# One attention and gated feed-forward layer: both chunks of the first sequence projected together through eight PSUM banks

## The chip, the cores and the metric

The kernel runs on one core of one Trainium2 chip. The metric is the device time of one execution in microseconds (us). Engines are named as the profile names them: PE (TensorE, matrix multiplications), ACT (ScalarE), DVE (VectorE), POOL (GpSimd), and SP, whose queue issues every DMA of this kernel.

## What is computed

Two sequences of 1024 tokens with 512 features are normalised, go through attention with 32 heads of 16 features (8 key/value groups) and, beside it, through a gated feed-forward layer with low-rank additions. The two results are multiplied and added to the input.

```python
x = L0_attn_x                                  # (2, 1024, 512), float32
xn = _layernorm(x, axis=-1)
s = attention(xn, Wq, Wkv, Wo, bo)             # causal, scores * 16**-0.5, softmax, context, Wo, + bo
gate = xn @ gate_w.T + (xn @ gate_a.T) @ gate_b.T      # 512 -> 1376, rank 16
up   = xn @ up_w.T   + (xn @ up_a.T)   @ up_b.T
hidden = silu(gate) * up
g = silu(hidden @ down_w.T + (hidden @ down_a.T) @ down_b.T)
out = x + s * g
```

## The kernel before, in words

**Precision.** Projections are made from a rounded high half and a low half of each operand: three matmuls (high by high, low by high, high by low; `matmul_hi_lo`, L240 to L242) for each 128 rows of the contraction. ACT writes the high half from a PSUM bank, DVE subtracts it from the value to get the low half.

**Tiling.** The 2048 tokens are four chunks `c` of 512 (0 and 1 are the first sequence, 2 and 3 the second). For a chunk there are: a layer norm on DVE (`layernorm`, L1239 to L1253) with one square root on ACT (`root`, L1031); four transposes `turn` (L809), of 4 blocks each; one projection for the keys (`KEYS_BLOCK`), four for the queries (`blk` 0 to 3), each of 12 matmuls of 512 columns; and `value` (L834), 16 small multiplications that the trace shows as 32 records. After a `turn`, ACT writes the unrounded `xT` (L1036, which `value` reads) and the high half `x_hi` (L1037), and DVE writes `x_lo` from them (L1259). Projections go to DRAM (`scratch_q`, `scratch_k`, L566) and values too (L571); they come back laid out for the heads (L738, L741, L745).

**Banks.** PSUM has eight banks of 512 columns: three for the scores `s`, two for the transposed scores `st`, one for the context `o`, and two (`bank0`, `bank1`) for everything that is not attention. `bank_places` hands these two out in turn; the next user of a bank waits (`take_bank`) until its last content was read, for a `turn` until `x_hi` is written, for a projection until `proj_lo` is.

**Order.** Each engine runs two streams: the background (turns, projections, values, then weights folded with their low-rank part in `fold` L847 and L851, then `hidden` L872, and later the output) and the attention, in 17 rounds of 40 slots. `interleave` first runs `LEAD` steps of the background alone, then gives so many steps to each slot. LEAD ended behind projection (1, 0), at step 36. Round -1 (the next 40 slots) takes another 30 steps (`EARLY`), and in it PE makes the scores of head group 0 (`score_pair`, L966, from slot 6 on) for the row maxima, which DVE takes (L1409 with the causal mask, L1412 without) and which are turned and stored as extra rows of `q` (L973, L753). With slot 0 of round 0 the transposed scores (L985) and the exponentials (L1191) begin. Behind round -1 every background step has its place by the same rule.

**The background's order up to there:** turn 0; then for chunks 0 to 3 the keys, the values, the turns of the next chunk, and one query projection (`BESIDE`); then two more query projections (`AFTER[:SOON]`), the two folds of the first weight tile, and `hidden`.

**Low-rank factors.** SP waits until all four values are stored (L658), then loads the raw factors `low_a_raw` and `low_b_raw` (L659, L660) into memory that the tiles of the first stage held, and behind them the first eight weight tiles (L594). ACT rounds both factors (`split_low`, L1058, L1059) and DVE takes their low halves (`low_of_low`, L1270, L1273). The first fold waits for both.

**The start of the attention.** SP's `LOAD` in slot 1 of round -1 waits until projections (0, 0), (1, 0) and the keys of chunk 1 are stored, then loads `k` and `q` of group 0 whole.

Of the kernel before, what the change touches and what calls it, by code (L numbers as in the profile page):

```python
# [80 lines left out]
LOAD = 1  # L81
# [13 lines left out]
PROJECTED = []  # L95
for _c in range(NCH):
    PROJECTED += [(_c, KEYS_BLOCK)] + BESIDE[_c:_c + 1]
PROJECTED += AFTER

# [10 lines left out]
SOON = 2  # L110
# [13 lines left out]
def bank_order():  # L124

    for k in range(KT):
        yield "turn", 0, k
    for c in range(NCH):
        yield "proj", c, KEYS_BLOCK
        yield "value", c, 0  # L130
        if c + 1 < NCH:
            for k in range(KT):
                yield "turn", c + 1, k
            yield ("proj", *BESIDE[c])
# [110 lines left out]
def layer(nc, x, Wq, Wkv, Wo, bo, gate_w, up_w, down_w, low_a, low_b, low_a_down, low_b_down, out):  # L245
# [5 lines left out]
    with ExitStack() as ctx:  # L251
# [35 lines left out]
        with ExitStack() as first:  # L287
# [6 lines left out]
            with ExitStack() as own:  # L294
                xT = sbuf(own, "xT", [P, KT, C])
# [7 lines left out]
            with ExitStack() as own:  # L303
                with ExitStack() as brief:
                    a_raw = sbuf(brief, "low_a_raw", [LR, 2, D])
# [3 lines left out]
                with ExitStack() as brief:  # L309
                    b_raw = sbuf(brief, "low_b_raw", [LR, 2, F])  # L310
                wh = sbuf(own, "w_hi", [P, 2, 2, KT, P], F32R)
                wl = sbuf(own, "w_lo", [P, 2, 2, KT, P], F32R)
                hid, hid_l = in_place(own, "hid", [P, 2, C], "_lo")
        x_in = ring[:, :, :].rearrange("p (a t) d -> p a t d", a=2)
# [45 lines left out]
        xT_hi = sem("xT_hi")  # L360
        xT_lo = sem("xT_lo")
        p_hi = sem("p_hi")
# [36 lines left out]
        loaded = [[sem(f"loaded{i}_{pair}") for pair in range(2)] for i in range(2)]  # L399
        v_loaded = [sem(f"v_loaded{i}") for i in range(3)]  # L400
# [25 lines left out]
        def bank_of(key):  # L426
            return bank[BANKS[key][0]]
# [7 lines left out]
        def read_out(kind, a, b):  # L435
# [4 lines left out]
            return dict(turn=(xT_hi, KT * a + b + 1), proj=(p_lo, (kind == "proj" and projection(a, b)) + 1), value=(v_copied, a + 1),  # L440
# [11 lines left out]

        def head_rows(h, n):
            return slice(64 * (h % 2), 64 * (h % 2) + n)
# [4 lines left out]
        def _(pool):  # L459
            pool.memset(prob[:, 0, 0], 0.0).then_inc(zero_made, 1)  # L460
# [46 lines left out]

            def background():
                done = 0
# [36 lines left out]
        def _(sp):  # L546
# [4 lines left out]

            def store_projection(c, blk):
# [3 lines left out]
                hi = ph[:, n % 2].bitcast(F32)  # L556
                lo = pl[:, n % 2].bitcast(F32)
# [16 lines left out]
            def load_raw(n):  # L574

                if n == 0:
                    wait_filled(sp, ("turn", NCH - 1, KT - 1))
# [64 lines left out]
            def background():  # L642
                yield KT * STEPS["turn"]
                load_x(2)
                for c in range(NCH):
# [4 lines left out]
                    if c + 1 < NCH:  # L650
                        yield KT * STEPS["turn"]
                        if c + 3 < NCH:
                            load_x(c + 3)
                        yield STEPS["proj"]
                        store_projection(*BESIDE[c])
                for i in range(2):
                    sp.wait_ge(v_stored[i], DMA * NCH // 2)
                sp.wait_ge(xn_ready, NCH)  # L658
                sp.dma_start(a_raw[:, :, :], low_a).then_inc(low_landed, DMA)  # L659
                sp.dma_start(b_raw[:, :, :], low_b).then_inc(low_landed, DMA)  # L660
                for n in range(8):
                    load_raw(n)
# [821 lines left out]
```

## Time and profile before

| what | us |
|---|---|
| median of 3 runs | 1012.03 (1011.39 to 1013.53) |
| the profiled execution | 1009.25 |
| its span, first to last instruction | 1007.5 |
| PE busy in the span | 925.6 (92%) |
| DVE / ACT / POOL busy | 584.2 / 486.1 / 304.1 |

The span is the time between the first and the last instruction of the profiled execution; 1.75 us of its time lie around it. Busy is the time in which an engine had at least one instruction running. A PE that is busy is not always at its full clock: the column PEclk of the table of windows gives the granted clock, 1.00 for 2.4 GHz and 0.50 for 1.2 GHz.

### The profile page before, as it was taken

The numbers are of one execution on the slowest core, as the hardware profiler recorded it, in microseconds if no ns is written. First come the engines' busy times: TensorE is split into PE (matmuls) and PEld (weight loads), VectorE is DVE, ScalarE is ACT, GpSimd is POOL, SyncE is SP. The second block draws the span as 40 slices with busy tenths as digits, with TensorE's granted clock in tenths as the row PEclk, the third lists the DMA queues.
The fourth block names the chain that finished last, engine by engine and source line by source line (L and its number), as shares of the span: only waits on it lengthen the run. The fifth ranks groups of instructions, "written<-read, shape, count | busy, mean of one in ns | idle before, by whom it ended". The sixth has DMA issues, their size and how long they took to land.

```text
span 1007.5 us, 18056 instructions
## 1 busy us (share of the span) xinstructions
PE 925.6 (92%) x6599; PEld 595.6 (59%) x6599; DVE 584.2 (58%) x1669; ACT 486.1 (48%) x975; POOL 304.1 (30%) x307
## 2 busy tenths in 40 slices
PE   4738699999999999999999999998999999989985
PEld 3625466666666666666666666554555555555664
DVE  6536656666666566665656575767655656640025
ACT  3402355656565556565656555656443443444211
POOL 3000023434343434343434343441111223120126
PEclk9967889999999999999999999999999999999999
DMA  6441724242424242424242433357745645335554
GB/s 230 150 110 44 248 86 136 76 143 79 141 81 133 84 129 86 122 87 122 90 117 96 120 100 116 91 143 218 204 116 157 178 143 141 91 94 155 156 158 151
DMA packets 142566, 129.01 MB, mean 128 GB/s; under 512 B 36104, under 2 KB 104296, under 8 KB 142256
## 3 DMA queue, kind: packets, MB, share of 16 engines
q1 hardware_dynamic: 142480, 127.87, 42.5%
q8 instruction: 54, 0.88, 0.4%
q14 instruction: 32, 0.26, 0.1%
HBM read 74.07 MB, written 53.22 MB: 126 GB/s over the span
## 4 chain that ended last, share of the span: by engine, by line
PE 79%; DVE 8%; DMA 4%; ACT 4%; issue 2%; SPq 2%; POOL 0%; POOLq 0%; DVEq 0%; ACTq 0%
PE bank L872 24%; PE o L1002 12%; PE bank L240 9%; PE s L966 9%; PE st L985 8%; PE bank L241 6%; PE bank L242 6%; DVE junk L1409 2%; PE bank L834 2%; DMA q<-scratch_q 2%; DVE neg_pad L1425 1%; PE bank L847 1%; PE bank L851 1%; DVE hid L1299 1%; DMA inv_sums<-scratch_r 1%
## 5 line engine op out<-in xcount | busy, mean ns | idle before, releaser
L1191 ACT ACTIVATE prob<-st 128x512 f32<-128x512 f32 (+1 forms) x640 | 324.3, 554 | 289.9 <-PE st L985 289.5
L1409 DVE CUSTOM_DVE_ANT_0 junk<-s,mask 128x128 bf16<-128x128 f32 (+3 forms) x512 | 229.4, 487 | 126.6 <-PE s L966 125.7
L1412 DVE TENSOR_REDUCE part_max<-s 128x1 f32<-128x512 f32 x256 | 163.7, 681 | 106.6 <-PE s L966 106.6
L484 POOL TENSOR_SCALAR_AFFINE_SELECT prob<-prob 128x512 f32<-128x512 f32 x128 | 84.2, 670 | 351.6 <-ACT prob L1191 351.1
L966 PE MATMUL s<-k,q 64*128 64x512 f32 (+3 forms) x768 | 150.3, 380 | 22.7 <-DMA q<-scratch_q 12.3
L872 PE MATMUL bank<-x_hi,w_hi 64*128 64x512 f32 (+1 forms) x704 | 151.0, 416 | 2.4 <-DVE hid L1299 1.1
L1002 PE MATMUL o<-prob,v 128*32 128x512 f32 (+3 forms) x1536 | 144.6, 494 | 0.0
L872 PE MATMUL bank<-x_lo,w_hi 64*128 64x512 f32 (+1 forms) x704 | 142.7, 392 | 0.0
L872 PE MATMUL bank<-x_hi,w_lo 64*128 64x512 f32 (+1 forms) x704 | 141.8, 390 | 0.0
L985 PE MATMUL st<-q,k 64*128 64x512 f32 (+3 forms) x768 | 136.6, 374 | 3.6 <-ACT prob L1191 3.6
L966 PEld LDWEIGHTS s<-k,q 64*128 64x128 f32 x768 | 77.4, 187 | 66.5 <-DVE part_max L1409 26.6
L493 POOL TENSOR_TENSOR tanh<-tanh,hid 128x512 f32<-128x512 f32 (+1 forms) x44 | 56.6, 1286 | 166.1 <-DVE hid L1299 166.1
L985 PEld LDWEIGHTS st<-q,k 64*128 64x128 f32 x768 | 71.8, 185 | 58.3 <-issue 35.1
L872 PEld LDWEIGHTS bank<-x_hi,w_hi 64*128 64x128 f32 (+1 forms) x704 | 68.7, 183 | 42.2 <-issue 32.2
L240 PE MATMUL bank<-down_hi,hid_in 128*128 128x512 f32 (+1 forms) x176 | 78.1, 444 | 2.9 <-issue 2.2
L501 POOL TENSOR_TENSOR hid_lo<-hid,tanh_hid_hi 128x512 fp32r<-128x512 f32 (+1 forms) x44 | 56.7, 1289 | 75.8 <-ACT tanh_hid_hi L1100 75.8
L1002 PEld LDWEIGHTS o<-prob,v 128*32 128x32 f32 x1536 | 39.5, 109 | 65.4 <-issue 61.3
L872 PEld LDWEIGHTS bank<-x_lo,w_hi 64*128 64x128 f32 (+1 forms) x704 | 68.6, 182 | 13.0
L872 PEld LDWEIGHTS bank<-x_hi,w_lo 64*128 64x128 f32 (+1 forms) x704 | 69.1, 183 | 7.5
L241 PE MATMUL bank<-down_lo,hid_in 128*128 128x512 f32 (+1 forms) x176 | 69.2, 393 | 0.0
L242 PE MATMUL bank<-down_hi,hid_in 128*128 128x512 f32 (+1 forms) x176 | 69.0, 392 | 0.0
L495 POOL TENSOR_TENSOR hid<-tanh,hid 128x512 f32<-128x512 f32 (+1 forms) x44 | 56.5, 1283 | 3.5
(103 smaller groups left out, 1004.1 us busy)
## 6 DMA issues: line engine op xcount, KB each, us to landing
hid_in<-scratch_hid SPq DMA_DIRECT2D x16, 1408.0 KB, 7.3
q<-scratch_q SPq DMA_DIRECT2D x64, 200.0 KB
scratch_hid<-tanh_hid_hi SPq DMA_DIRECT2D x40, 256.0 KB, 2.1
scratch_hid<-hid_lo SPq DMA_DIRECT2D x40, 256.0 KB, 2.4
scratch_q<-proj_hi SPq DMA_DIRECT2D x32, 256.0 KB
scratch_o<-o_sb SPq DMA_DIRECT2D x32, 256.0 KB
k<-scratch_k SPq DMA_DIRECT2D x32, 192.0 KB
scratch_q<-proj_lo SPq DMA_DIRECT2D x16, 256.0 KB
```

The lines of the kernel that those rows point to most:

```text
L240: pe.matmul(out, lhs_hi, rhs_hi, start=start, stop=False)
L241: pe.matmul(out, lhs_hi, rhs_lo, start=False, stop=False)
L242: return pe.matmul(out, lhs_lo, rhs_hi, start=False, stop=stop)
L484: ins = pool.affine_select(out=blk, in_=blk, compare_op=ALU.is_ge, fill=0.0, base=0, pattern=[[0, REP], [1, P]], channel_multiplier=-1)
L501: pool.tensor_tensor(hid_l[0:hp, n % 2], hid[0:hp, n % 2], hid_h[0:hp, n % 2], ALU.subtract)\
L872: mm = pe.matmul(bank[i][0:hp, :], w_[half, h % 2, i, kt, 0:hp], x_[half, c, kt], start=not cross and kt == 0 and w_ is wh and x_ is xh, s ...
L966: pe.matmul(sb_[(p + odd) % S_BANKS][:, 0:wd], q[half, g % 2, h // 2, qt * P:(qt + 1) * P], k[half, g % 2, k0:k0 + wd], start=True, stop=T ...
L985: mm = pe.matmul(st[odd][:, col:col + q1 - q0], k[half, i % 2, kt * P:(kt + 1) * P], q[half, i % 2, h // 2, q0:q1], start=True, stop=True)
L1002: mm = pe.matmul(ob[32 * h:32 * h + 2 * HD, q0 % C:q0 % C + q1 - q0], v[:, i % 3, kt].rearrange("p a e -> p (a e)"), prob[:, job % 3, h, c ...
L1191: nc.scalar.activation(prob[:, job % 3, h, 0:JOB_COLS[j]], st[at % ST_BANKS][:, 0:JOB_COLS[j]], ACT.Exp, scale=float(HD) ** -0.5).then_inc ...
L1409: ins = dve.tensor_tensor_reduce(junk[:, n % S_BANKS, 0:wd], bank_[:, 0:wd], mask[:, C - wd:C], 1.0, LOWEST, ALU.add, ALU.max, part[:, h, ...
L1412: ins = dve.tensor_reduce(part[:, h, qt, dst:dst + 1], bank_[:, 0:wd], AX.X, ALU.max)
```

## The change

- **Order.** `LEADING` is new: the turns of chunks 0 and 1, then keys and query block 0 of chunk 0 and of chunk 1, then the values of both. Behind it come, for chunks 2 and 3, the turns, one query projection of chunk 0 or 1 (block 1), the keys, the values. `SOON` goes from 2 to 1. LEAD ends behind the same projection (1, 0), which now is step 24; EARLY is 42 steps. The total is the same.
- **Banks.** The eight turns of chunks 0 and 1 take all eight banks, one each; DVE's `x_lo` is now made from the bank. A turn's bank is free when `xT` is copied, which for chunks 0 and 1 happens apart from the rounding and later (`round_x`, `copy_x`); `xT` has two halves for it.
- **POOL** takes over the low halves of the key weights, of the query weights (in four pieces, `low_query_weights`) and of `x` for chunks 2 and 3 (`low_x` in the POOL block). ACT rounds the query weights in four pieces.
- **Buffers.** The third and fourth projection (keys and block 0 of chunk 1) are written to the buffers of the exponentials (`prob`), which nothing uses at that time. So are the raw low-rank factors, loaded at the program's start. ACT rounds `bT` behind the square root of chunk 3 (`split_low_b`) and `low_a` once all values are stored (`split_low_a`).
- **Loads.** `x` of chunk 1 is loaded ahead of `wkv`. `load_first` brings the first 512 columns of `k` and `q` of group 0 as soon as chunk 0's two projections are stored; `LOAD` brings the rest, and the values of a group are loaded in slot 19 rather than slot 1. The first eight weight tiles are loaded four at a time, behind the turns of chunk 2 and of chunk 3.
- **Layer norms** of chunks 0 and 1 follow each other on DVE; chunk 2's stands behind the eight `x_lo`, chunk 3's behind `proj_lo` of (0, 0).

```diff
-LOAD = 1
+LOAD, LOAD_V = 1, 19
...
-BESIDE = [(0, 0), (1, 0), (0, 1)]
-AFTER = [(1, 1), (0, 2), (1, 2), (0, 3), (1, 3)] + [(c, blk) for blk in range(NBLK - 1) for c in (2, 3)]
...
+LEADING = [(c, blk) for c in range(2) for blk in (KEYS_BLOCK, 0)]
+BESIDE = {2: (0, 1), 3: (1, 1)}
+AFTER = [(0, 2), (1, 2), (0, 3), (1, 3)] + [(c, blk) for blk in range(NBLK - 1) for c in (2, 3)]
+PROJECTED = LEADING + [p for c in BESIDE for p in (BESIDE[c], (c, KEYS_BLOCK))] + AFTER
...
-SOON = 2
+SOON = 1
...
-    last, turn, places, prior = [None, None], 0, {}, {}
+    last, turn, places, prior = [None] * 8, 0, {}, {}
...
+        elif u < 8:
+            used = (u,)
...
+            def load_first():
...
+                for a in range(2):
+                    sp.wait_ge(p_stored[a], 3 * DMA)
+                sp.wait_ge(zero_stored, DMA * (B + 2))
+                for h in range(2):
+                    sp.dma_start(k[head_rows(h, ROWS), 0, 0:C].bitcast(F32), k_dram[0][:, 0:C]).then_inc(first_loaded[0], DMA)
+                for h in range(REP):
+                    sp.dma_start(q[head_rows(h, AUG), 0, h // 2, 0:C].bitcast(F32), q_dram[h][:, 0:C])\
+                        .then_inc(first_loaded[h // 2], DMA)
...
+            sp.dma_start(a_raw, low_a).then_inc(low_landed, DMA)
+            sp.dma_start(b_raw, low_b).then_inc(low_landed, DMA)
...
+            def split_low_a():
+                for i in range(2):
+                    act.wait_ge(v_stored[i], DMA * NCH // 2)
+                act.wait_ge(xn_ready, NCH)
+                nc.scalar.activation(a_gu[:, :, :], a_raw, ACT.Copy).then_inc(low_hi, 1)
...
+                for c, blk in LEADING:
+                    if c == 1 and blk == KEYS_BLOCK:
+                        root(3)
+                        split_low_b()
+                        for kt in range(KT):
+                            copy_x(1, kt)
+                    yield STEPS["proj"]
+                    split_projection(c, blk)
```

**ACT at the start.** Before, from the first square root to the first copy of the values; `small` is the square root, `xT` and `x_hi` are the two copies of a turned bank.

```order
L1031 ACTIVATE small<-small 128x4
L1118 ACTIVATE wk_hi<-wkv 128x512
L1036 ACTIVATE xT<-bank 128x512
L1037 ACTIVATE x_hi<-bank 128x512
...
L1031 ACTIVATE small<-small 128x4
L1124 ACTIVATE wq_hi<-wq 128x2048
L1045 ACTIVATE proj_hi<-bank 128x512
L1052 ACTIVATE v_sb<-bank 128x4x8x16
```

Now ACT, from behind the copies of chunk 0 to the projections of chunk 1, with the banks' numbers:

```order
L1100 ACTIVATE small<-small 128x4
L1125 ACTIVATE proj_hi<-bank0 128x512
L1125 ACTIVATE proj_hi<-bank1 128x512
L1100 ACTIVATE small<-small 128x4
L1138 ACTIVATE bT<-prob 96x2752
L1112 ACTIVATE xT<-s2 128x512
L1112 ACTIVATE xT<-st0 128x512
```

The square root of chunk 3, the rounding of `bT` and the last four copies now stand between the projections of chunk 0 and those of chunk 1.

**PE around the first scores.** Before, the scores begin beside the values of chunk 1:

```order
L834 MATMUL bank<-wkv,xT 128x128 x4
L966 MATMUL s<-k,q 128x128 x2
L834 MATMUL bank<-wkv,xT 128x128 x4
L966 MATMUL s<-k,q 128x256 x2
L966 MATMUL s<-k,q 128x384 x2
L834 MATMUL bank<-wkv,xT 128x128 x4
```

Now PE, at the same slots:

```order
L896 MATMUL bank<-wkv,xT 128x128 x28
L1035 MATMUL s<-k,q 128x128 x2
L896 MATMUL bank<-wkv,xT 128x128 x4
L1035 MATMUL s<-k,q 128x256 x2
L867 MATMUL bank<-ident,ring 128x128 x4
L1035 MATMUL s<-k,q 128x384 x2
```

Seven of the eight value steps of chunks 0 and 1 now stand ahead of the first score, and the turns of chunk 2 beside the next ones. From the first transposed scores (`st`) on, PE's rows are the same in both programs.

**DVE ahead of the folds.** Before, behind the last query projection of round -1 (`low_a`, `bT` are the low halves of the two factors):

```order
L1265 TENSOR_TENSOR proj_lo<-bank,proj_hi 128x512
L1270 TENSOR_TENSOR low_a<-low_a_raw,low_a 32x1024
L1273 TENSOR_TENSOR bT<-low_b_raw,bT 32x2752
L1409 ISA junk,part_max<-s,mask 128x512
```

Now DVE, at the end of the values of chunk 3:

```order
L1519 TENSOR_REDUCE part_max<-s 128x1 x2
L1380 TENSOR_TENSOR low_a<-prob,low_a 32x1024
L1516 ISA junk,part_max<-s,mask 128x384
L1516 ISA part_max 128x1
```

The low half of `low_a` moved ahead of three pairs of maxima, and that of `bT` to the end of the lead.

## Rows read from the trace of the kernel before

**Rows 1.** Busy time by window: us, PE, PEld, DVE, ACT, POOL, PEclk, DMA share, GB/s

```profile
12.40:71.30 58.90, 36.40 (x180) 29.53 (x180) 31.02 (x73) 18.34 (x35) 0.00 (x0) 0.87 0.44 137
71.30:105.60 34.30, 28.92 (x133) 19.91 (x133) 21.08 (x67) 6.30 (x12) 0.00 (x0) 0.78 0.26 77
105.60:132.10 26.50, 17.67 (x80) 10.54 (x79) 15.61 (x36) 12.19 (x17) 3.51 (x3) 0.78 0.79 254
132.10:181.70 49.60, 49.12 (x414) 33.14 (x414) 30.03 (x90) 26.99 (x55) 15.49 (x16) 0.98 0.34 98
```

**Rows 2.** Chain of work, 0 to 120 us: start, duration, engine, tile, line

```profile
12.43 1.10 PE bank L809 x4
...
20.40 0.43 PE bank L240
...
24.24 3.88 PE bank L834 x32
...
30.21 0.49 ACT x_hi L1037
...
33.38 2.39 DVE stats L1239 x4
...
39.73 0.61 DVE proj_lo L1265
...
59.24 5.59 DMA scratch_q<-proj_lo
...
66.15 5.12 DMA q<-scratch_q
...
71.31 0.47 PE s L966 x2
...
94.27 0.23 PE bank L240
```

**Rows 3.** Busy time by window inside round -1, columns as in rows 1

```profile
71.30:80.00 8.70, 8.07 (x34) 6.35 (x34) 3.64 (x16) 0.04 (x1) 0.00 (x0) 0.54 0.37 119
80.00:88.00 8.00, 4.67 (x28) 2.75 (x28) 6.05 (x23) 4.80 (x9) 0.00 (x0) 0.89 0.15 35
88.00:93.00 5.00, 5.00 (x14) 3.10 (x13) 2.15 (x7) 0.27 (x1) 0.00 (x0) 0.50 0.01 3
```

**Rows 4.** Timeline ahead of the first fold: start, us, engine, line, tile [idle before]

```profile
106.26 0.38 SPq L571 DMA_DIRECT2D scratch_v<-v_sb  x1
...
109.00 0.35 SPq L659 DMA_DIRECT2D low_a_raw<-in_low_a  x1
...
117.42 1.06 ACT L1058 ACTIVATE low_a<-low_a_raw 96x1024 fp32r<-96x1024 f32 x1 [1.12 <-DMA low_b_raw<-in_low_b]
...
118.38 2.48 ACT L1059 ACTIVATE bT<-low_b_raw 96x2752 fp32r<-96x2752 f32 x1
...
118.51 1.22 DVE L1270 TENSOR_TENSOR low_a<-low_a_raw,low_a 32x1024 fp32r<-32x1024 f32 x1 [1.49 <-ACT low_a L1058]
...
120.89 3.02 DVE L1273 TENSOR_TENSOR bT<-low_b_raw,bT 32x2752 fp32r<-32x2752 f32 x1 [1.17 <-ACT bT L1059]
...
124.01 1.09 PE L847 MATMUL bank<-ident,ring 128*128 128x128 f32 x4 [7.68 <-issue]
```

**Rows 5.** DVE's groups by form, 0 to 100 us, POOL idle from 10 us on

```profile
L1259 DVE TENSOR_TENSOR x_lo<-xT,x_hi 128x512 fp32r<-128x512 f32 x16 | 11.1, 691 | 15.0 <-ACT x_hi L1037 15.0
...
L1409 DVE CUSTOM_DVE_ANT_0 junk<-s,mask 128x512 bf16<-128x512 f32 x4 | 2.6, 687 | 1.7 <-PE s L966 1.7
...
L1425 DVE TENSOR_TENSOR neg_pad<-neg_max,neg_pad 128x16 fp32r<-128x16 f32 x1 | 0.2, 175 | 0.0
```

**Rows 6.** DVE's groups by form, 140 to 190 us, POOL at work

```profile
L1409 DVE CUSTOM_DVE_ANT_0 junk<-s,mask 128x512 bf16<-128x512 f32 x8 | 5.2, 687 | 1.2 <-PE s L966 1.2
...
L1425 DVE TENSOR_TENSOR neg_pad<-neg_max,neg_pad 128x16 fp32r<-128x16 f32 x2 | 1.3, 666 | 0.1
```

**Rows 7.** POOL's groups by form, 120 to 180 us

```profile
L493 POOL TENSOR_TENSOR tanh<-tanh,hid 128x512 f32<-128x512 f32 x3 | 3.9, 1284 | 11.1 <-DVE hid L1299 11.1
```

More of the change, by code:

```diff
@@ L124, in bank_order @@
 def bank_order():
-    for k in range(KT):
-        yield "turn", 0, k
-    for c in range(NCH):
+    for c in range(2):
+        for k in range(KT):
+            yield "turn", c, k
+    for c, blk in LEADING:
+        yield "proj", c, blk
+    for c in range(2):
+        yield "value", c, 0
+    for c in BESIDE:
+        for k in range(KT):
+            yield "turn", c, k
+        yield ("proj", *BESIDE[c])
         yield "proj", c, KEYS_BLOCK
         yield "value", c, 0
[L131 to L134, printed above, removed]
     for c, blk in AFTER[:SOON]:
@@ L399, in layer @@
         loaded = [[sem(f"loaded{i}_{pair}") for pair in range(2)] for i in range(2)]
+        first_loaded = [sem(f"first_loaded{pair}") for pair in range(2)]
         v_loaded = [sem(f"v_loaded{i}") for i in range(3)]
@@ L439, in read_out @@
                 return (gate_read, NCH * a + b + 1), (up_read, NCH * a + b + 1)
-            return dict(turn=(xT_hi, KT * a + b + 1), proj=(p_lo, (kind == "proj" and projection(a, b)) + 1), value=(v_copied, a + 1),
+            return dict(turn=(xT_copied, KT * a + b + 1), proj=(p_lo, (kind == "proj" and projection(a, b)) + 1), value=(v_copied, a + 1),
                         fold=(w_lo, 2 * a + b + 1), down_fold=(d_lo, a + 1), down=(y_done, a + 1),
@@ L555, in store_projection @@
                 sp.wait_ge(p_lo, n + 1)
[L556 to L557 removed]
+                hi, lo = (tile.bitcast(F32) for tile in projected(n))
                 if blk < KEYS_BLOCK:
@@ L642, in background @@
             def background():
-                yield KT * STEPS["turn"]
-                load_x(2)
-                for c in range(NCH):
+                for c in range(2):
+                    yield KT * STEPS["turn"]
+                    load_x(2 + c)
+                for c, blk in LEADING:
+                    yield STEPS["proj"]
+                    store_projection(c, blk)
+                    if (c, blk) == (0, 0):
+                        load_first()
+                for c in range(2):
+                    yield STEPS["value"]
+                    store_value(c)
+                for c in BESIDE:
+                    yield KT * STEPS["turn"]
+                    for n in range(4 * (c - 2), 4 * (c - 2) + 4):
+                        load_raw(n)
+                    yield STEPS["proj"]
+                    store_projection(*BESIDE[c])
                     yield STEPS["proj"]
@@ L1129, in background @@
                     copy_value(c)
-                    if c + 1 < NCH:
-                        for kt in range(KT):
-                            yield STEPS["turn"]
-                            copy_x(c + 1, kt)
-                        if c + 2 < NCH:
-                            root(c + 2)
-                        yield STEPS["proj"]
-                        split_projection(*BESIDE[c])
+                split_low_a()
                 for c, blk in AFTER[:SOON]:
@@ L1188, in exponential @@
                 act.wait_ge(st_done, at + 1)
+                if job == 0 and h == 0:
+                    for a in range(2):
+                        act.wait_ge(p_stored[a], 2 * 3 * DMA)
+                if job == 1 and h == 0:
+                    act.wait_ge(low_lo, 2)
                 if h == 0 and job >= 3:
```

214 lines of the change are left out of this document (131 added, 83 removed).

## The prediction, made before the changed kernel was timed

> **What bounds the kernel now.** I read the busy time by window first, then the chain of waits of the first 120 us, then the timeline where PE stands still. From 132.1 us on PE is busy 49.1 of 49.6 us [rows 1]: nothing there can be gained by moving waits, and PE's row order there is the same in both programs, as it is from the first transposed scores on. So the change can only move the moment at which `hidden` starts, at 132.1 us now. Ahead of it PE is busy 36.4 of 58.9 us, 28.9 of 34.3 and 17.7 of 26.5 [rows 1], partly at a granted clock of 0.5. Three losses can be seen. (a) The lead: first score at 71.31 us, the last 12 us of it a store (5.6) and a load (5.1) in DRAM, one behind the other [rows 2]. (b) Round -1 up to the values of chunk 3, 71.3 to 105.6: the work is there, but 0.54 and 0.50 of the clock in two stretches and 3.3 us idle in the third [rows 3]. (c) The first fold waits 7.7 us for the low-rank factors, which are loaded only when all values are stored [rows 4].
>
> I build the new program's times from the trace's durations, up to the same mark, the start of `hidden`.
>
> **The lead.** The first four turns start at 12.4 as before. Cold turns cost 1.0 to 1.1 us [rows 2], without a bank to wait for they end at 16.5. A layer norm takes 6.35 us on DVE (33.38 to 39.73 [rows 2]) and chunk 1's can start at 12.3; but ACT's square root now stands behind four roundings that end at 17.0, 1.6 us later than DVE needs it, so `xn` of chunk 1 is ready at 20.3.
>
> POOL's subtraction of the first query weights falls on the rest of this norm. In the trace the small two-input subtraction `neg_pad` takes 0.175 us with POOL idle and 0.666 on average with POOL at work [rows 5, 6]; a POOL subtraction of this size takes 1.28 [rows 7]. I take 1.1 us here, between 0 and 2.6 (both early POOL subtractions in full): ready at 21.4. The masked maximum, whose inputs are one bank and one tile in SBUF, takes 0.687 in both places [rows 5, 6]; so I add nothing for POOL's eight `x_lo`.
> The Trainium skill, "SBUF — State Buffer", section Who interferes with whom, speaks against moving the low halves to POOL: a DVE instruction with two SBUF inputs waits for a GpSimd one that reads SBUF, and with one such input it does not. By that rule the sum would be the same as by these rows; the trace agrees with both halves of it.
>
> Four turns to 25.4, rounding to 26.0, the first copy to 26.6, and the first projection starts (the bank of the first turn is free only then). Twelve matmuls at 0.43 [rows 2] end at 31.8, the next three projections at 0.23 [rows 2], 2.8 us each, at 34.6, 37.4 and 40.2. Then the values of chunk 0 need the bank of chunk 1's keys. Those wait on ACT: `proj_lo` of (0, 0) is done at 35.8, the norm of chunk 3 has its variance at 38.9, the square root ends at 39.1, `bT` takes 2.5 [rows 4], four copies 0.5 each [rows 2], rounding 0.6, `proj_lo` 0.7: 44.9. PE stands 4.7 us, so a new stall takes the place of an old one. 56 of the 64 value records must run ahead of the first score: 6.8 us at 3.88 for 32 [rows 2], and 2.7 more for a cold clock (twelve matmuls at 0.43 rather than 0.23 are 2.4; a little more): **first score at 54.5**. Its data are earlier: projection (0, 0) is stored from 36.8, 5.6 us of store and 5.1 of load behind issues of 2.3 give about 49. The other half is stored from 47.6, loaded from 53 and there at 59, and PE asks for it at about 64. So the lead gives 71.3 - 54.5 = 16.8.
>
> **Round -1 up to the values of chunk 3.** PE's rows there at full clock: one value step and two values 8.7, eight turns 4.8 (0.6 each, the 1.10 of [rows 2] at twice the clock and a little), four projections 11.0, 21 pairs of scores and a turn of the maxima 8.3 (0.4 each; the pair at 71.31 took 0.47 cold [rows 2]): 32.8 us. By the same count the old stretch has 21.4 and took 34.3, 12.9 lost: about 4 in the cold restart (in my 2.7 above already), 4 in the turns of chunk 3 (80 to 88, PE busy 4.7 of 8.0), 2.5 in the cold stretch behind them [rows 3], the rest waits on DVE. The new stretch has two such phases of turns, each without four `x_lo` of 0.69 on DVE [rows 5], which stood between the maxima. I take 8 lost, 2 for each phase, 1.5 cold, 2.5 waits; from below 3, from above 18 (the old loss and another phase at its old price). 40.8 us, values of chunk 3 at 95.3 against 105.6: 6.5 of the 16.8 are given back.
>
> **Up to the fold.** Before, 18.4 us from the values of chunk 3 (105.6) to the first fold (124.01 [rows 4]). Now the factors are there; what is left is the copy 0.6, the store from 0.4 us issue to landing at 109.0 (2.7), `low_a` on ACT 1.06 and on DVE 1.22 [rows 4]: 6.2. ACT and DVE stand still in this chain, in order, and behind them the first exponentials, three pairs of maxima and the next projection's halves; PE runs dry after 2.8 us of its rows and resumes at about 6.8. Its rest ahead of the fold is 2.7: **fold at 9.5 behind the values, 104.8**. The loads of group 1, which stood behind 3.4 MB in the queue, no longer do. From fold to `hidden` it was 8.0 us at 0.5 of the clock [rows 1, 4]; at full clock 6, after a 4 us stall I take 7: 111.8. The eight weight tiles are loaded at the turns of chunks 2 and 3, beside 30 us of PE work; should that cover fail, a wait of up to their transfer comes back, about 8 us for 2 MB at 254 GB/s [rows 1].
>
> **Sum.** `hidden` at 111.8 against 132.1: 20 us less (16.8 - 6.5 + 8.9 + 1.0). The profiled execution's 1009.25 (1007.5 of it span) becomes 989; the median of the runs lies 2.8 above it, so **992 us**.
>
> **Rivals.**
> *The early stage stays bound by the clock and DVE* (chance 0.17). The two phases of turns leave PE sparse, as 80 to 88 did, and each brings 5 us at half clock, or POOL does hold up the maxima (eight times 1.28 us, 10.2). For it: PE idles 4.7 us right ahead of this stage. Against: `x_lo` is off DVE, and the maximum shows no slowing. The loss is 18, not 8: 1002 us.
> *Less is lost* (0.12). Clock up all the way, 3 lost in round -1, no stall at the fold (4 less, and 1 cold): 10 more, 982; with half of it 986.
> *It gets slower* (0.03). One mechanism: the granted clock falls in the 4.7 us gap at 40 us and does not rise until the fold, since PE never gets dense enough. 45.6 us of full-rate work would take as much again, less the 4 or so counted: about +40, 1032. It decides from 20 us of work done at half rate beyond my sum. The trace has 0.54 for 8.7 us and 0.50 for 5 [rows 3], each time over within 9 us of work, which speaks against it.
> *The change does not do what it says* (0.04): eight banks fill PE early, but the first score still waits for its data, because `load_first` or its stores stand behind the 1.4 MB of factors and the zeros. With the first score at 71 as before, 40.8 and 16.5 give `hidden` at 128.6: 1008.6.
>
> **How the numbers follow.** Forecast 0.64, centre 992, its own range 987 to 998 (1 to 3 us on each of lead, round -1 and fold). The range that should hold 8 in 10 takes in most of the two near rivals: 984 to 1003. A measurement of this kernel tells 0.2% (2 us) from no change. Faster than 1010: forecast, both near rivals and half of the fourth case, 0.95; within 2 us 0.02, slower 0.03.
>
> **What would show it right or wrong.** Chain and timeline of after: the first turn of chunk 1 near 21.4; PE idle between the fourth projection and the first value, released by `proj_lo` of chunk 1's keys, 4 to 5 us; first score at 53 to 57; the end of the values of chunk 3 at 92 to 99; `low_a` on ACT straight behind a store of values; the first `hidden` matmul at 109 to 115; and from there the same length for each round as before, PE busy over 49 of 49.6 us [rows 1]. A granted clock of 0.5 between 60 and 95 us for more than 5 us would be the first rival; a first score released by the load of `q` would be the last; a first fold that waits for weight tiles would cost the fourth step. If the rounds behind `hidden` are longer or shorter than before, the argument that only the start moves is wrong.

## The result: 984.9 us, and where the 27 us came from

| | before | after |
|---|---|---|
| median of 4 runs | 1011.71 us (1011.10 to 1013.53) | 984.94 us (983.97 to 989.02) |
| after / before | | 0.974 (0.972 to 0.976) |
| the profiled execution | 1009.25 | 989.02 |
| its span | 1007.5 | 987.3 |
| first score | 71.31 | 51.95 |
| last values end, `hidden` starts | 105.6, 132.1 | 88.5, 106.09 |

The changed kernel is 2.6% faster, 26.8 us against 20 forecast, inside the range of 984 to 1003 but at its lower edge, and below the 987 to 998 that the forecast gave itself. `hidden` starts 26.0 us earlier, which is nearly what the medians differ by. The profiled execution shows only 20.2 us less: 3.2 of the missing 5.8 us are a fall of the clock behind 600 us, which is told below.

Busy time by window in the profiled execution of after (columns as in [rows 1], and the same cuts: the lead, round -1 up to the values of chunk 3, up to `hidden`, one round):

```profile
12.43:51.95 39.52, 28.70 (x138) 24.97 (x138) 29.26 (x67) 16.52 (x30) 3.81 (x3) 0.83 0.59 187
51.95:88.51 36.56, 35.26 (x197) 24.32 (x197) 23.77 (x77) 12.40 (x23) 12.49 (x10) 1.00 0.64 202
88.51:106.09 17.58, 11.62 (x59) 7.13 (x59) 7.90 (x22) 8.99 (x15) 0.63 (x1) 0.81 0.51 151
106.09:155.70 49.61, 49.15 (x416) 32.43 (x416) 30.83 (x93) 27.79 (x58) 16.56 (x18) 1.00 0.36 99
```

Against [rows 1] the lead is 58.9 → 39.5 us, round -1 34.3 → 36.6 although PE is busy 6 us more in it, at a clock of 1.00 rather than 0.78, and runs 197 matmul records rather than 133, and the end 26.5 → 17.6. The rounds behind it are the same: ten of them, counted from the 41st exponential on ACT to the 441st, take 498.2 us before and 498.6 after.

The chain of waits of after, up to `hidden` (start, duration, engine, tile, line; to be read beside [rows 2]):

```profile
20.88 1.12 PE s L867 x4
...
25.82 0.77 PE bank L246
26.59 0.43 PE bank L247
...
34.93 2.39 DVE stats L1345 x4
...
38.16 2.39 ACT bT L1138
40.55 1.93 ACT xT L1112 x4
...
43.83 8.12 PE bank L896 x56
51.95 0.26 PE s L1035 x2
...
88.51 0.61 ACT v_sb L1132
89.14 4.30 DMA scratch_v<-v_sb
...
93.51 1.07 ACT low_a L1144
94.60 1.22 DVE low_a L1380
...
96.56 0.80 PE s L1035 x2
...
101.36 0.84 PE bank L909 x4
...
106.09 0.91 PE bank L934 x6
```

The chain no longer holds the DRAM pair of [rows 2] (5.59 and 5.12 us). In its place, ahead of the values, stands a chain of layer norm, `bT`, four copies and a rounding, and behind the values a store of 4.30 us with `low_a` on ACT and DVE. The waits of 12 to 115 us name the same two places (waiting instruction, releaser: us in total, times, longest us):

```profile
PE s L1035 <- DVE part_max L1516: 6.0, 2, 5.7
...
PE bank L896 <- DVE prob L1374: 4.8, 1, 4.8
ACT low_a L1144 <- DMA scratch_v<-v_sb: 4.4, 1, 4.4
```

**The part that is not the change.** Two windows of after, far behind the changed part:

```profile
656.00:660.00 4.00, 3.24 (x16) 2.06 (x16) 3.54 (x12) 2.02 (x6) 0.00 (x0) 0.78 0.67 182
660.00:664.00 4.00, 4.00 (x15) 2.22 (x13) 2.32 (x11) 1.68 (x3) 0.63 (x1) 0.50 0.91 292
```

In a second profile of the same kernel (982.9 us of span, below) both windows have 1.00. From `hidden` to the end it took 877.2 us there, 881.2 in the first profile, 875.4 before. Later profiles lie between 877 and 883. Of the 13 profiles of this study 8 have a fall of the clock at this place, each 552 to 556 us behind the start of `hidden`; one of the 8 is the kernel before with early factors. The one profile of the kernel before has none, nor has the second one of the changed kernel, so the place is the program's, and whether the clock falls there differs between executions. So differences of up to 6 us between single executions arise behind `hidden`, and the experiments are read by their medians and, up to `hidden`, by their marks.

### The profile page after: what moved, and what is told of

The parts are those of the page before. It is cut to its first block, busy times and chain, and to the rows that moved or that the text cites. A ratio compares the mean times of both kernels' runs of the same rounds, so it can differ in the third digit from the quotient of the medians.

```text
span 987.3 us, 18068 instructions
## 1 busy us (share of the span) xinstructions
PE 927.0 (94%) x6599; PEld 598.5 (61%) x6599; DVE 576.7 (58%) x1659; ACT 487.5 (49%) x978; POOL 318.1 (32%) x320
## 4 chain that ended last, share of the span: by engine, by line
PE 84%; DVE 8%; ACT 3%; DMA 2%; issue 2%; POOL 0%; SPq 0%; POOLq 0%; DVEq 0%; ACTq 0%
PE bank L934 24%; PE o L1071 12%; PE bank L246 9%; PE s L1035 9%; PE st L1054 9%; PE bank L247 7%; PE bank L248 7%; DVE junk L1516 2%; PE bank L896 2%; DVE neg_pad L1532 1%; PE bank L909 1%; PE bank L913 1%; DVE hid L1406 1%; DMA inv_sums<-scratch_r 1%; ACT gate L1168 1%
## 5 line engine op out<-in xcount | busy, mean ns | idle before, releaser
L246 PE MATMUL bank<-down_hi,hid_in 128*128 128x512 f32 (+1 forms) x176 | 79.2, 450 | 3.0 <-issue 2.3
L248 PE MATMUL bank<-down_hi,hid_in 128*128 128x512 f32 (+1 forms) x176 | 69.9, 397 | 0.0
```

The lines of the kernel that those rows point to most:

```text
L246: pe.matmul(out, lhs_hi, rhs_hi, start=start, stop=False)
L248: return pe.matmul(out, lhs_lo, rhs_hi, start=False, stop=stop)
```

## Experiments

Each was run beside the kernel before on the same chip, three rounds or more. "Marks" are the first score, the last value step (the start of its last record, 0.3 us before the values end), the first fold and the first `hidden` matmul of the profiled execution. All are made from the changed kernel except one, which says so. The ratios compare the means of the runs; a distance from the changed kernel that is taken from them differs by up to 3 us from that between the medians, which the text gives (4.8 rather than 7.5 us for `x_lo` on DVE).

| run | median us | ratio to before | marks |
|---|---|---|---|
| changed kernel again | 985.22 | 0.974 (0.971 to 0.977) | 51.4, 87.7, 101.3, 105.7 |
| factors late | 999.14 | 0.987 (0.982 to 0.991) | 48.0, 89.6, 111.5, 118.9 |
| before, factors early | 1014.06 | 1.001 (0.998 to 1.004) | 72.1, 106.8, 126.1, 134.3 |
| two banks | 996.91 | 0.984 (0.980 to 0.989) | 54.6, 93.2, 106.9, 111.8 |
| `x_lo` on DVE | 992.67 | 0.979 (0.975 to 0.983) | 52.7, 96.5, 110.2, 114.7 |
| whole load | 998.88 | 0.986 (0.983 to 0.989) | 59.0, 98.8, 112.6, 117.6 |
| keys first | 985.48 | 0.973 (0.971 to 0.976) | 49.8, 89.2, 103.0, 107.7 |
| `low_a` early | 980.25 | 0.969 (0.966 to 0.972) | 50.1, 87.0, 93.5, 98.5 |
| lead and fold | 988.66 | 0.976 (0.973 to 0.979) | 55.4, 95.2, 101.7, 109.2 |
| POOL's piece later | 987.44 | 0.977 (0.974 to 0.980) | 51.4, 91.5, 105.2, 110.1 |
| POOL's piece and the wait | 982.68 | 0.971 (0.969 to 0.973) | 49.5, 86.9, 93.4, 100.2 |

### The changed kernel again

> The changed kernel again, on the chip of the next three. hidden at 106 us, stall of 5 to 6 us between the last values and the first fold, then half clock for about 5 us; median 984 to 988, single runs up to 5 us apart by falls of the clock behind 600 us, which the first three theories do not touch.

985.22 us (984.73 to 989.60), the same as the first time. This profile's span of 982.9 is the reference for the marks below.

### Which parts carry the gain

**The low-rank factors.** Loads, roundings and low halves go back behind the values and the query projection that follows them, as in the kernel before:

```diff
-            sp.dma_start(a_raw, low_a).then_inc(low_landed, DMA)
-            sp.dma_start(b_raw, low_b).then_inc(low_landed, DMA)
...
+                for i in range(2):
+                    sp.wait_ge(v_stored[i], DMA * NCH // 2)
+                sp.wait_ge(p_lo, 4)
+                sp.dma_start(a_raw, low_a).then_inc(low_landed, DMA)
+                sp.dma_start(b_raw, low_b).then_inc(low_landed, DMA)
...
-                        split_low_b()
...
-                split_low_a()
...
+                split_low_b()
+                split_low_a()
```

> The changed kernel with one part undone: the two raw low-rank factors are loaded by SP behind the store of the last values and rounded behind the first query projection of AFTER, as before; all else is the changed kernel. My theory (the early factors are worth the chain that stood ahead of the first fold): nothing moves until the values of chunk 3 end near 88.5 us; then store 4.9, load about 8, ACT 2.5, DVE 3.0 and 1.2 put the first fold at 107 to 110 rather than 101.4 and hidden at 112 to 115 rather than 106.0; the whole 7 us slower, about 992. Rival (the factors were hidden behind the load of group 1 and the weight tiles anyway): the fold stays at 101 to 103, the whole within 2 us of 985.

999.14 us, 14 more than the changed kernel where 7 were expected. The values now start at 40.1 us, as `bT` is not ahead of the copies, and the first score stands at 48.0 rather than 51.4. That gain is gone at once: PE then waits for the second half of `q`, and reads half clock for the window behind it (waits, and a window of this kernel):

```profile
PE s L1038 <- DMA q<-scratch_q: 2.8, 1, 2.8
```
```profile
64.00:68.00 4.00, 4.00 (x12) 2.75 (x11) 0.80 (x5) 0.13 (x1) 0.00 (x0) 0.50 0.96 310
```

At the fold it loses 10 us, and 3 more at half clock up to `hidden` (timeline of PE and ACT: start, us, line, tiles, idle before and what ended it):

```profile
111.53 1.08 PE L912 MATMUL bank<-ident,ring 128*128 128x128 f32 x4 [16.77 <-issue]
```
```profile
104.31 2.50 ACT L1141 ACTIVATE bT<-prob 96x2752 fp32r<-96x2752 f32 x1 [9.58 <-DMA prob<-in_low_b]
```

So the early factors are worth 14 us in the new order (12 by the ratios).

**The same part alone, in the kernel before**: the raw factors in the exponentials' buffers, loaded at the start, `bT` rounded in the lead, `low_a` once the values are stored.

```diff
+            sp.dma_start(a_raw, low_a).then_inc(low_landed, DMA)
+            sp.dma_start(b_raw, low_b).then_inc(low_landed, DMA)
...
-            for i in range(2):
-                sp.wait_ge(v_stored[i], DMA * NCH // 2)
-            sp.dma_start(low_a_raw, low_a).then_inc(low_landed, DMA)
-            sp.dma_start(low_b_raw, low_b).then_inc(low_landed, DMA)
```

> The kernel before with that one part alone: raw factors loaded at the start into the exponentials' buffers, bT rounded behind the turns of chunk 2, low_a once all values are stored. My theory: the 7.7 us stall ahead of the first fold goes and the clock no longer falls there; first fold at about 116.5 rather than 124.0, hidden at 121 to 124 rather than 132.1; 1002 (1000 to 1004). Rival: the stall only changes its name (the weight tiles or the load of group 1 are as late as the factors were): fold at 121 to 124, 1009 to 1012.

1014.06 us, no gain where 10 us were expected. The stall of 7.68 us in [rows 4] did go. A shorter one begins 7 us earlier, at 108.9, as ACT and DVE now wait in order for the last value to be stored (timeline of PE, then ACT; then two of three windows):

```profile
112.94 0.79 PE L962 MATMUL s<-k,q 64*128 64x512 f32 x2 [4.05 <-DVE part_max L1412]
```
```profile
110.16 1.06 ACT L1060 ACTIVATE low_a<-prob 96x1024 fp32r<-96x1024 f32 x1 [2.46 <-DMA scratch_v<-v_sb]
```
```profile
113.00:117.00 4.00, 4.00 (x10) 2.17 (x10) 2.07 (x7) 0.00 (x0) 0.00 (x0) 0.50 0.74 278
...
121.00:125.00 4.00, 4.00 (x12) 2.31 (x11) 1.68 (x4) 1.08 (x2) 0.00 (x0) 0.52 0.72 198
```

Behind it PE has rows without a pause and runs them at 1.2 GHz for about 12 us; in the kernel before the same rows ran at 2.4 GHz, and PE stood idle afterwards. The idle time was traded for the same time at half clock: the first fold came at 126.1 rather than 124.0. This is the clearest lesson of the study. A price per part, 14 us in one order and nothing in the other, does not exist here.

**Eight banks.** Back to two, with rounding and copy of each turn together, `x_lo` from `xT`, and the norm of chunk 1 behind the four `x_lo` of chunk 0:

```diff
-        elif u < 8:
-            used = (u,)
...
                 layernorm(0)
-                layernorm(1)
                 for c in range(2):
                     for kt in range(KT):
                         yield STEPS["turn"]
                         low_x(c, kt)
+                    if c == 0:
+                        layernorm(1)
```

> The changed kernel with the turns of chunks 0 and 1 on two banks again, so each copy stands beside its rounding and DVE takes x_lo of chunk 0 ahead of the norm of chunk 1, from xT; the order of projections, values and loads is the changed one. My theory (the order and the early half load bring most of the lead's gain, the eight banks a part): first projection at 30 to 31 us rather than 25.8, the gap ahead of the values shrinks from 4.75 to 2 to 3 because the copies of chunk 1 are done, first score at 55 to 58 rather than 51.9, the whole 3 to 6 us slower, 988 to 991. Rival A (the banks carry the gain): first score at 65 to 71, 998 or more. Rival B (banks are worth nothing, the layer norm rules): first score within 1 us, 985.

996.91 us, 12 more (10 by the ratios) where 3 to 6 were expected. The first score is 3.2 us later, `hidden` 6.1; the other 4.5 of its profiled execution fall behind `hidden`, where single executions differ as much. What costs the first microseconds is the norm of chunk 1, which stands behind four `x_lo` here: PE waits 9.17 us for it rather than 4.81, and the turns of chunk 1 start at 26.0 rather than 20.8 (timeline of PE):

```profile
26.02 1.97 PE L865 MATMUL bank<-ident,ring 128*128 128x128 f32 x8 [9.17 <-DVE ring L1353]
```

So 6 us are shown for this edit, the banks and the place of the norm together. Two banks with the norm of chunk 1 first were not tried, so what the banks alone are worth is not shown.

**`x_lo` of chunks 2 and 3 on DVE rather than POOL:**

```diff
-                        low_x(c, kt)
...
-                    yield KT * STEPS["turn"]
+                    for kt in range(KT):
+                        yield STEPS["turn"]
+                        dve.wait_ge(xT_copied, KT * c + kt + 1)
+                        dve.tensor_tensor(xl[:, c, kt], xT[:, c % 2, kt], xh[:, c, kt], ALU.subtract).then_inc(xT_lo_late, 1)
```

> The changed kernel with x_lo of chunks 2 and 3 on DVE again, between the maxima. The prediction's step (without these four subtractions in each phase of turns DVE does not hold PE up, and the clock stays): 0.69 x 4 more on DVE in each phase, the stretch from the first score to the end of the values of chunk 3 takes 39 to 43 us rather than 36.6, possibly with a fall of the clock; the whole 3 to 6 us slower, 988 to 991. Rival (PE's own rows fill this stretch, DVE has room for 5.5 us more): within 1 us of 36.6, the whole 985.

992.67 us, 7.5 more. The stretch from the first score to the last value takes 43.8 us against 36.3. (The first score itself is 1.3 us later, ahead of anything that the edit touches; the two intervals of the ratio overlap, so it is the marks that tell the runs apart.) Two of its windows (the third, to 68 us, reads like the second):

```profile
56.00:60.00 4.00, 2.18 (x11) 1.46 (x11) 3.58 (x11) 2.23 (x5) 0.00 (x0) 0.77 0.45 173
60.00:64.00 4.00, 4.00 (x14) 2.28 (x12) 2.45 (x10) 1.08 (x2) 0.00 (x0) 0.50 0.50 130
```

The eight subtractions are 5.5 us of DVE (0.69 each). What they cost is that PE starves during the turns (2.18 of 4 us, DVE 3.58) and works at half clock for the next 10 us. This is the state in which the kernel before was ([rows 3]), and which the move to POOL ended.

**The load in halves.** Without `load_first`; group 0 comes whole when chunk 1 is stored:

```diff
-                    if (c, blk) == (0, 0):
-                        load_first()
...
-                        cols = slice(0, T) if g else slice(C, T)
+                        cols = slice(0, T)
...
-                    pe.wait_ge(first_loaded[h // 2], (2 if h else 4) * DMA)
+                    pe.wait_ge(loaded[0][h // 2], (2 if h else 4) * DMA)
```

> The changed kernel without load_first: k and q of group 0 come whole, behind the stores of all four leading projections, as before. Theory (in the changed kernel the first score comes 19 us earlier mainly because its data no longer wait for chunk 1): stores of (1, 0) issued by about 48, landed at 53 to 55, load 5 to 7: first score at 60 to 63 rather than 51.9, PE idle and then at half clock, hidden at 114 to 118, 993 to 998. Rival (the order alone brings it and the early half load hides behind the values): first score within 2 us, 985 to 987.

998.88 us, 14 more than the changed kernel. PE waits 8.8 us for `q`, the first score starts at 59.0, and 56 to 68 us run at half clock (waits, then one of the three windows):

```profile
PE s L1033 <- DMA q<-scratch_q: 8.8, 1, 8.8
```
```profile
60.00:64.00 4.00, 4.00 (x17) 2.89 (x17) 1.25 (x7) 1.57 (x3) 0.00 (x0) 0.50 0.46 105
```

A first score 7.6 us later became a `hidden` 11.9 us later.

Taken out one at a time, the four parts cost 14, 12, 7.5 and 14 us, 47 together, of a gain of 27: they are not to be added. The order of the projections, the earlier weight tiles, the later load of a group's values and POOL's low halves of the weights were not taken out, so their share is not shown.

### The two stalls that the prediction named

**The gap ahead of the values.** The square root of chunk 3, `bT` and the norm go behind the keys of chunk 1, which the values wait for:

```diff
                     if c == 1 and blk == KEYS_BLOCK:
-                        root(3)
-                        split_low_b()
                         for kt in range(KT):
                             copy_x(1, kt)
...
+                root(3)
+                split_low_b()
...
-                    if (c, blk) == (0, 0):
-                        layernorm(3)
+                layernorm(3)
```

> The changed kernel with the norm of chunk 3, its square root and the rounding of bT behind the projections of chunk 1 rather than ahead of them. Theory A (what the run with late factors showed: from there on the loads rule): the gap of 4.75 us ahead of the values goes, but the first score waits for q until about 48, and the second half of q, whose stores stand behind load_first in SP's queue, until about 62; PE is idle 2 to 5 us there and the clock falls; hidden at 104 to 107, no gain to speak of (984 to 988). Theory B (the gap alone held the lead): first score at 46 to 48, hidden 4 to 6 us earlier, 979 to 981.

985.48 us, the same as without the edit. The gap ahead of the values (4.75 us) is gone, they start at 39.0, and PE waits 4.4 us for `q` instead (timeline of PE, then a window):

```profile
49.76 0.48 PE L1035 MATMUL s<-k,q 64*128 64x128 f32 x2 [4.38 <-DMA q<-scratch_q]
```
```profile
48.00:52.00 4.00, 2.25 (x10) 2.07 (x10) 3.35 (x5) 0.14 (x1) 0.00 (x0) 0.61 0.52 162
```

The windows up to 60 us read 0.50 and 0.61. The stall only changed its place and its name.

**The wait for the store of the values.** ACT takes `low_a` as soon as the last low halves of `x` are made. The wait for the stored values moves to the first rounding of a folded weight (`w_hi`, in `split_weight`): `w_hi` lies over `v_sb`, which the store reads, and `low_a` only over the front part of `xT`:

```diff
-                for i in range(2):
-                    act.wait_ge(v_stored[i], DMA * NCH // 2)
+                act.wait_ge(xT_lo_late, 2 * KT)
...
+                if (h, i) == (0, 0):
+                    for a in range(2):
+                        act.wait_ge(v_stored[a], DMA * NCH // 2)
```

> The changed kernel, but ACT rounds low_a as soon as the values of chunk 3 are computed and POOL has taken the last x_lo; the wait for the stored values stands ahead of the first rounded weights instead. Theory (the stall ahead of the fold is the in-order wait of ACT and DVE for a store, not PE's work): the stall falls from 5.7 to about 1 us, the clock does not fall there, first fold 8 to 9.5 us behind the last values rather than 12.9, hidden at 97 to 101 rather than 106.0, 977 to 981. Rival (the stall moves on to the weight tiles or to the store ahead of the first rounded weights): hidden at 103 to 106, 983 to 985.

980.25 us (979.01 to 984.13; the changed kernel beside it 984.73 to 989.60): the fastest kernel of the study. `low_a` stands straight behind the copy of the last value. The stall of PE, 5.71 us in the first profile of the changed kernel and 6.24 in the second, is 1.19, and the clock does not fall (timeline of ACT, of PE, then a window):

```profile
87.34 0.60 ACT L1132 ACTIVATE v_sb<-bank 128x512 f32<-128x512 f32 x1 [4.73 <-PE bank L896]
87.83 1.05 ACT L1143 ACTIVATE low_a<-prob 96x1024 fp32r<-96x1024 f32 x1
```
```profile
90.87 0.49 PE L1035 MATMUL s<-k,q 64*128 64x512 f32 x2 [1.19 <-DVE part_max L1518]
```
```profile
92.00:96.00 4.00, 3.98 (x29) 2.85 (x27) 2.96 (x10) 2.87 (x6) 0.63 (x1) 1.00 0.67 196
```

From the last value step to `hidden` it is 11.5 us rather than 18.0. Taking 5 us out of the stall gave 6.5 up to `hidden`, and 5 in the median.

**Both stalls, and POOL's piece later.** The norm and square root of chunk 3 behind the projections as in *keys first*, `bT` rounded ahead of the roundings of chunk 1's turns, `low_a` early, POOL's first piece of the query weights behind the norm of chunk 1, and `load_first` issued behind the stores of chunk 1 (with semaphores of their own for those):

```diff
-                    if (c, blk) == (0, 0):
-                        load_first()
+                load_first()
...
                 round_query_weights(0)
+                split_low_b()
...
-                        layernorm(3)
...
+                layernorm(3)
```

> Both together, and more: bT rounded in ACT's idle time behind the norm of chunk 1; DVE's half of it behind proj_lo of (0, 0); norm of chunk 3 behind the projections; POOL's query weights behind the norm of chunk 1; chunk 1's projections stored ahead of load_first, on semaphores of their own, so that the second half of q comes early; low_a early as in the run before. Theory: first turn of chunk 1 at 19.9 (without POOL's 1.0), values right behind the projections at 38, first score when its data land, 48 to 49, second half there before 58, last values at 84 to 86, hidden at 92 to 96, 971 to 976, faster than both. Rival (DVE becomes the bound of round -1, or the denser queue delays the first half): first score after 51 or last values after 88, 979 or more.

988.66 us where 971 to 976 were expected: no faster than the changed kernel (985.22; their runs overlap), and 8 slower than `low_a` early alone. PE waited 9.0 us for `q`, and 56 to 64 us read 0.50; SP had issued its loads late (timeline of SP):

```profile
38.15 1.88 SPq L620 DMA_DIRECT2D scratch_q<-proj_lo  x1
40.07 4.33 SPq L620 DMA_DIRECT2D scratch_k<-prob  x3
44.45 3.77 SPq L620 DMA_DIRECT2D scratch_q<-prob  x3
48.34 2.07 SPq L602 DMA_DIRECT2D k<-scratch_k  x2
```

The first scattered stores of this kernel took 0.6 us of issue each, those issued with others still running 0.9 to 1.9. The six of chunk 1, next to those of chunk 0, took 8.1 us, and the loads stood behind them. `bT` took a part too: ACT waited 3.79 us for the raw factors ahead of it, and the first projection started at 26.64 rather than 24.83 as with POOL's piece alone.

### POOL beside DVE

POOL waits for chunk 1's norm before it subtracts the first query weights:

```diff
+                pool.wait_ge(xn_ready, 2)
                 low_query_weights(0)
```

> The changed kernel, POOL's first piece of the low query weights waits until the norm of chunk 1 is done. Theory (POOL's subtraction holds up one small DVE instruction of that norm, 1.17 us instead of 0.17): that instruction takes 0.17 again, the first turn of chunk 1 starts at 19.9 rather than 20.9, the first score and hidden come 1 us earlier (105), the whole 984; too little for the whole time to tell, the rows tell it. Rival (the long instruction has another cause): it stays at 1.17.

987.44 us, against 985.22 in another batch (the ratios overlap): not told apart. The mechanism did what was meant. First the changed kernel (timeline of DVE, then of POOL), then this one (DVE):

```profile
17.50 1.17 DVE L1356 TENSOR_SCALAR small<-small 128x4 f32<-128x4 f32 x1
```
```profile
17.39 1.26 POOL L534 TENSOR_TENSOR wq_lo<-wq,wq_hi 128x512 fp32r<-128x512 f32 x1 [3.46 <-ACT wq_hi L1117]
```
```profile
17.51 0.17 DVE L1357 TENSOR_SCALAR small<-small 128x4 f32<-128x4 f32 x1
```

The first turn of chunk 1 starts at 19.89 rather than 20.88. The values start no earlier all the same, at 45.0: they wait for the norm of chunk 3, which stands behind that of chunk 2, and chunk 2's `x` landed late in this execution. The chain of waits of this kernel has the first row, that of the next one, whose start is the same program, has the second:

```profile
16.11 12.38 DMA ring<-in_L_attn_x
```
```profile
16.11 8.98 DMA ring<-in_L_attn_x
```

3.4 us between two executions of one load is more than the 1 us of lead that was to be shown. The profiled execution is also the slowest of its four (993.27).

**With `low_a` early as well** (this diff and that of *`low_a` early* together):

> low_a rounded early together with the later query weights. Theory: 1 us on the first score, hidden at 97 to 98, 979 against 980.2 of low_a alone. Rival (the first score is held by the load of q by then): hidden at 98.5, 980.

982.68 us (982.26 to 983.50). The first score at 49.5 is the earliest but one, yet the end is no better than with `low_a` early alone (ratio 0.971 against 0.969, intervals overlapping). In the profiled execution PE waits at 97 us for the `q` of group 1. There is no gain to be shown for the piece.

## Why the prediction held, and where its sizes were off

The direction, the range and the mechanism held: only the start of `hidden` moved, the DRAM pair left the chain, and the two new stalls stood where they were named. The sizes were less good. The first score (51.95), the end of the values (88.5) and `hidden` (106.1) all came earlier than the brackets set for them (53 to 57, 92 to 99, 109 to 115).

**The lead (16.8 forecast, 19.4 measured).** Norm of chunk 1 at 21.4: 20.88. The square root waited behind the roundings for 1.63 us as said, and one small instruction was held by POOL, 1.17 rather than 0.17 us; I had taken 1.1 for it. Here I had to judge from a two-input subtraction, and what was held is an instruction with one input. The Trainium skill, "SBUF — State Buffer", section Who interferes with whom, lists `tensor_scalar` among those that can enter a mode with two ports and contend; the trace agrees, by its 1.17 us beside POOL and 0.17 us alone. Four projections to 40.2: to 39.08. The gap by `proj_lo` of chunk 1's keys 4.7: 4.75. The projections ended 1.1 us earlier than forecast, and "2.7 more for a cold clock" was mis-sized: the 56 value records took 8.12 us, 1.3 above their 6.8. Together they put the first score at 51.95 and not at 54.5.

**Round -1 (40.8 forecast, 36.6 measured).** The trace has the rows that I had counted (8 turns, 4 projections, 72 value records, 21 pairs of scores); against my 32.8 us for them "8 lost" was 3.8. PE was idle for only 1.3 of it; the other 2.5 lie in the rows themselves, which took longer than I had priced them although the clock was full. I had priced two phases of turns at 2 each and 1.5 for a cold stretch. The clock was 1.00 from 48 to 92 us, and PE was dense in both phases of turns, of which these are the windows:

```profile
56.00:60.00 4.00, 3.65 (x20) 2.21 (x19) 2.39 (x12) 2.54 (x5) 4.00 (x4) 1.00 0.29 111
...
72.00:76.00 4.00, 3.52 (x20) 2.17 (x20) 3.08 (x10) 3.78 (x8) 2.98 (x3) 1.00 0.60 150
```

My argument was right, that four `x_lo` on DVE were what starved PE in the turns; with them back on DVE the stretch takes 43.8. But I let half of the old loss stand after I had removed its cause. The two are coupled: without the starving the clock does not fall, and both losses go together.

**From the values to the fold (9.5 forecast, 12.9 measured).** The mechanism was named: `low_a` behind the store, ACT and DVE in order behind it, PE dry. Two sizes were short. The store took 4.30 us (4.85 in the second profile) where [rows 4] gave me 2.7. And I had taken the 2.7 us of rows behind it at full clock; they took 4.8 at half:

```profile
92.00:96.00 4.00, 0.00 (x0) 0.00 (x0) 1.37 (x2) 2.46 (x3) 0.00 (x0) 0.88 0.54 147
96.00:100.00 4.00, 3.44 (x8) 2.14 (x8) 2.17 (x6) 0.96 (x2) 0.00 (x0) 0.50 0.60 176
```

Why the store took longer was not tested: all transfers together moved 231 GB/s around its start (88 to 92 us), and 165 around that of the one before (105 to 109). From fold to `hidden` it was 4.7 us and not 7: the clock was back by 102.

**The factors' worth** was 8.9 in my sum, all of it at the fold. The run with the factors late gives 14 in the new order, the run of the kernel before with them early gives none. A term of a sum can't carry both; it held here because the other parts of the change were there too.

**The rivals.** Less is lost (982, 0.12) is nearer to the measured 984.9 than the forecast of 992 is. It was right for round -1, where 3 lost were its number and 3.8 were measured, and wrong at the fold, where it had no stall. The stage bound by clock and DVE is what `x_lo` on DVE shows, at 992.7 rather than the 1002 that I gave it. That `load_first` is late is what *lead and fold* shows. The slower one, a clock that falls at 40 us and stays down, did not happen: behind the gap it read 0.59 for 4 us, then 1.00.

```profile
44.00:48.00 4.00, 4.00 (x23) 4.00 (x24) 3.97 (x2) 1.00 (x2) 1.27 (x1) 0.59 0.30 87
```

**The sum.** `hidden` 26 us earlier, not 20: 2.6 more in the lead, 4.2 in round -1, 3.4 less at the fold, 2.3 more behind it, about 6 in all. The rounds behind are unchanged, as said. That the profiled execution took the forecast 989 is luck: `hidden` began 5.7 us earlier than forecast, and the rest took 5.8 us longer than before, by the fall of the clock (3.2) and small differences in the late rounds and the end.

## What to carry to other kernels

Price a stall with the half clock that it leaves behind, not by its length: a wait of 4 us in front of dense work cost as much as a wait of 8 us further on (*before, factors early*), and an engine that starves PE during a sparse phase costs more than its own time. When two in-order engines must wait for a store, put the wait at the instruction that overwrites the data, not at the first one that is near. And before a stall is removed, look up when the next input arrives: the gap ahead of the values could go only up to the load of `q`, so removing it gave nothing.

## What the runs showed of the hardware that I had not expected

**Idle time and the clock.** Ahead of the turns of chunk 1 PE stood still for 4.81 us in both profiles of the changed kernel, and the first projection behind them ran at half clock. In three other profiles whose program is the same up to there (*whole load*, *keys first*, *`low_a` early*) it stood still for the same 4.81 us, and the first projection ran at full clock. First the window of the changed kernel (its first profile), then that of *`low_a` early*:

```profile
24.00:28.00 4.00, 2.73 (x8) 1.98 (x7) 3.84 (x7) 2.89 (x6) 0.00 (x0) 0.50 0.64 197
```
```profile
24.00:28.00 4.00, 2.73 (x13) 1.95 (x12) 3.84 (x7) 2.88 (x6) 0.00 (x0) 1.00 0.52 161
```

The matmuls of the first projection followed each other at 0.43 us in the one and at 0.23 in the other. With 9.17 us of idle time (*two banks*) it was 0.23 too, and with 3.81 us it was 0.23 (*POOL's piece later*) and, behind 3.08 us more, 0.43 (*lead and fold*). So the length of the idle stretch does not decide it; what does is open. The difference moves the start of the values by 1.2 us (42.28 in *`low_a` early*, 43.48 in the second profile of the changed kernel), and so stands in the marks of single profiles. The clock's column can't be trusted this early: it reads 1.00 from 20 to 24 us in the kernel before, where these matmuls follow each other at 0.43 [rows 2].

How long the half clock lasted behind an idle stretch was not the same either: 5 us behind 5.7 us of idle time in the changed kernel, 12 us behind 4.05 us of it in the kernel before with early factors, both with PE busy throughout. What decides that is open.

**The issue of a store was slower with stores outstanding**, up to 1.9 us rather than 0.6 (*lead and fold*), so SP's order counted even where no transfer was on the path. That the outstanding stores are the cause was not tested.
